# A graph network on one core: the fourth edge stage with gathered queries, two sum banks and no loop

## What is computed

```python
q = (tfn_features @ Wq).reshape(n, H, DQK)              # 8 heads of 16
x_dst = tfn_features[edge_dst]
wk = mlp2(edge_features, k_w1, k_b1, k_w2, k_b2)        # per edge, 128 wide
wv = mlp2(edge_features, v_w1, v_b1, v_w2, v_b2)
k = tensor_product(x_dst, edge_sh, wk, Cqk)             # wk * sum_s sh[s] * (x @ C[:, s])
v = tensor_product(x_dst, edge_sh, wv, Cv)              # 9 harmonics s
attn = jnp.einsum('ehd,ehd->eh', q[edge_src], k)
ex = jnp.exp(attn - segment_max(attn, edge_src)[edge_src])
alpha = ex / (segment_sum(ex, edge_src)[edge_src] + 1e-16)
upd = segment_sum(v * alpha[..., None], edge_src)
out = tfn_features @ W_self + upd.reshape(n, OV) @ W_out
return (out - mu) * jax.lax.rsqrt(var + EPS_BN) * gamma + beta
```

## Time and profile before

| | us |
|---|---|
| median of three runs | 3519.25 |
| lowest and highest | 3516.62, 3521.51 |
| the profiled execution, its own time | 3510.65 |
| its span in the profile | 3508.9 |
| mean granted TensorE clock over the span | 0.805 |

### The profile page before, as it was taken

One profiled execution on the slowest core, in us unless ns is written; L12 is line 12 of the kernel. 1 busy time (PEld: TensorE's weight loads), 2 busy tenths in 40 slices (PEclk: granted clock), 3 DMA queues, 4 the chain that ended last, 5 costly groups with the idle time before them and its releaser, 6 DMA issues. The chain is left out here.

```text
span 3508.9 us, 58176 instructions
## 1 busy us (share of the span) xinstructions
PE 2551.3 (73%) x14132; PEld 2166.8 (62%) x14132; DVE 2280.8 (65%) x5044; ACT 1062.1 (30%) x2723; POOL 1789.0 (51%) x1813
## 2 busy tenths in 40 slices
PE   3778777514554444357777765999999999999986
PEld 2778776413443333245555544888888888888872
DVE  3555555337887887855556542677777777777775
ACT  1111111134554564111111101344444344443441
POOL 2777776066666663157777723444444344443400
PEclk7776777556555666589999967999999999999985
DMA  2443443265554552035445517988888888888830
GB/s 64 93 87 84 87 87 64 46 161 131 132 123 125 132 124 72 2 110 157 153 153 161 158 63 177 203 204 197 197 201 199 200 198 190 193 200 198 195 92 9
DMA packets 433884, 475.50 MB, mean 136 GB/s; under 512 B 200837, under 2 KB 304648, under 8 KB 433712
## 3 DMA queue, kind: packets, MB, share of 16 engines
q1 hardware_dynamic: 358832, 295.60, 35.9%
q0 software_dynamic: 59904, 123.64, 15.2%
q10 hardware_dynamic: 14976, 54.53, 4.5%
HBM read 408.18 MB, written 65.34 MB: 135 GB/s over the span
## 5 line engine op out<-in xcount | busy, mean ns | idle before, releaser
L1960 PE MATMUL psum<-ckv,z 128*128 128x256 f32 x4160 | 969.7, 384 | 0.0
L1960 PEld LDWEIGHTS psum<-ckv,z 128*128 128x128 f32 x4160 | 767.9, 191 | 98.5
L1823 POOL DMA_INDIRECT ga<-XX,src_i x416 | 398.1, 957 | 449.7 <-PE psum L1941 307.0
L985 POOL DMA_INDIRECT ga<-T,src_i x416 | 431.4, 1037 | 302.3 <-issue 112.5
L275 POOL DMA_INDIRECT ga<-T,src_i x416 | 401.3, 965 | 151.7 <-issue 124.4
L275 POOL DMA_INDIRECT ga<-TA,src_i x416 | 412.4, 991 | 126.7 <-issue 126.7
L2009 DVE TENSOR_TENSOR z<-psum,shb 128x2560 f32<-128x2560 f32 x104 | 293.7, 2824 | 125.8 <-PE psum L1941 78.5
L455 PE MATMUL psum<-wre,re 128*128 128x68 f32 x832 | 213.4, 349 | 142.1 <-DVE oneT L331 82.6
L1816 POOL TENSOR_TENSOR acc<-acc,wkv 128x512 f32<-128x512 f32 x104 | 114.3, 1099 | 332.7 <-DMA wkv<-WKV 316.4
L455 PEld LDWEIGHTS psum<-wre,re 128*128 128x128 f32 x832 | 173.4, 258 | 162.9 <-issue 153.9
L2050 DVE TENSOR_TENSOR acc<-acc,psum 128x256 f32 x416 | 175.4, 422 | 120.2 <-PE psum L1932 90.9
(11 more groups left out here) (349 smaller groups left out, 4862.8 us busy)
## 6 DMA issues: line engine op xcount, KB each, us to landing
shb<-in_ea SPq DMA_DIRECT2D x104, 640.0 KB
WKV<-wkvo ACTq DMA_DIRECT2D x104, 512.0 KB
shb<-in_ea SPq DMA_DIRECT2D x104, 512.0 KB
wkv<-WKV SPq DMA_DIRECT2D x104, 512.0 KB
dl<-DL SPq DMA_DIRECT2D x312, 128.0 KB, 3.5
acc<-QW SPq DMA_DIRECT2D x416, 64.0 KB
win<-TB SPq DMA_DIRECT2D x416, 32.0 KB
ga<-T,src_i POOLq DMA_INDIRECT x832
```

What stands on the lines that cost most here:

```text
L985: pool.indirect_dma_start(ga[:, ring(g) + t, :], None, T1, bass.IndirectOffsetOnAxis(ap=src_i[:, g * GT + t:g * GT + t + 1], axis=0)).then ...
L1823: pool.indirect_dma_start(ga[:, (g % GR) * GT + t, :], None, XX, bass.IndirectOffsetOnAxis(ap=src_i[:, g * GT + t:g * GT + t + 1], axis=0) ...
L1960: last = pe.matmul(kv_of(k)[:, t, :], z[:, k % 2, j, t * 128:(t + 1) * 128], ckv[:, j, :], start=(j == 0), stop=(j == NZ - 1))
```

## The change

Queries: SyncE's `dl` and window loads go, and with them ScalarE's `places` and `queries` and TensorE's `queries`. GpSimd instead gathers each edge's row of QW by its destination, one indirect DMA a tile, into `qg`, a ring of four groups (QR), one group behind the XX gathers. GpSimd's multiply goes; VectorE makes it at the head of `keys_and_values`. The destinations of padding edges are clamped to 0 ahead of the stage. Sums: half 1 goes to bank 1, which the queries leave free, and each half waits only for the adds of the same half of the group before. Loop: `each_step` writes all 14 rounds out on every engine that used it. The diff, its removed and added lines with some of their surroundings:

```diff
@@ -1678,7 +1678,7 @@
-        QW = dram("QW", [NW, F])
+        QW = dram("QW", [N, F])
@@ -1697,13 +1697,12 @@
-                sp.dma_start(QW[N:NW, :], zero[:, 0:F]).then_inc(n3_o, 16)
-                sp.dma_start(QW[0:N, :].rearrange("(j p) f -> p j f", p=PN), tab[:]).then_inc(n3_o, 16)
-                sp.wait_ge(n3_o, 4 * 16)
+                sp.dma_start(QW.rearrange("(j p) f -> p j f", p=PN), tab[:]).then_inc(n3_o, 16)
+                sp.wait_ge(n3_o, 3 * 16)
             @block.gpsimd
@@ -1728,6 +1727,7 @@
             def _(dve):
+                c.link(dve.tensor_scalar(dst_i[:], dst_i[:], 0, None, ALU.max))
             @block.scalar
@@ -1756,14 +1756,13 @@
-        WR = 2
-        e3_w = [sem(f"e3_w{k}") for k in range(WR)]
+        QR = 4
+        e3_gq = [sem(f"e3_gq{k}") for k in range(UG)]
-        e3_dl = [sem(f"e3_dl{k}") for k in range(2)]
-        (e3_one, e3_oa, e3_oT, e3_ta, e3_X, e3_z, e3_Q, e3_q, e3_wq, e3_V, e3_ev, e3_s, e3_S, e3_acc, e3_M, e3_Mx, e3_i,
-         e3_pad, e3_sp) = [sem("e3_" + x) for x in
-            ("one", "oa", "oT", "ta", "X", "z", "Q", "q", "wq", "V", "ev", "s", "S", "acc", "M", "Mx", "i", "pad", "sp")]
+        (e3_one, e3_oa, e3_X, e3_z, e3_wq, e3_V, e3_ev, e3_s, e3_S, e3_acc, e3_M, e3_Mx, e3_i, e3_pad) = [
+            sem("e3_" + x) for x in
+            ("one", "oa", "X", "z", "wq", "V", "ev", "s", "S", "acc", "M", "Mx", "i", "pad")]
@@ -1771,7 +1770,6 @@
-        dl = tmp("dl3", [128, 2, GT * W], BF16)
@@ -1783,12 +1781,12 @@
-        oneT = acc[:, 2, 0:2 * GT * W].rearrange("p (a e) -> p a e", a=2)
-        qs = acc[:, 2, 2 * GT * W:4 * GT * W].rearrange("p (a e) -> p a e", a=2)
-        win = acc[:, 2, 4 * GT * W:4 * GT * W + WR * GT * F].rearrange("p (t f) -> p t f", f=F)
+        qg = acc[:, 2, 0:QR * GT * F].rearrange("p (t f) -> p t f", f=F)
+        sums_of = lambda half: bank[1] if half else bank[6]
+
         def soft_1(i, k):
@@ -1801,19 +1799,19 @@
         def each_step(eng, body):
-            each_group(eng, body)
-            for k in range(UG):
-                body(NI, k)
+            for i in range(NI + 1):
+                for k in range(UG):
+                    body(i, k)
             @block.gpsimd
             def _(pool):
-                def weighted_query(g):
-                    slot = g % 2
-                    pool.wait_ge(e3_q, g + 1)
-                    pool.wait_ge(e3_n[slot], (g // 2 + 1) * 16)
-                    q = qs[:, slot, :].rearrange("p (t f) -> p t f", t=GT)
-                    pool.tensor_tensor(q, q, wkv[:, slot, :, 0:F], ALU.mult).then_inc(e3_wq, 1)
+                def queries(g):
+                    if g >= QR:
+                        pool.wait_ge(e3_ev, (g - QR + 1) * 2)
+                    for t in range(GT):
+                        pool.indirect_dma_start(qg[:, (g % QR) * GT + t, :], None, QW, bass.IndirectOffsetOnAxis(
+                            ap=dst_i[:, g * GT + t:g * GT + t + 1], axis=0)).then_inc(e3_gq[g % UG], 16)
                 groups = NT // GT
                 for g in range(groups):
@@ -1822,19 +1820,15 @@
-                    if g > GR:
-                        weighted_query(g - GR - 1)
-                for g in range(groups - GR - 1, groups):
-                    weighted_query(g)
+                    if g:
+                        queries(g - 1)
+                queries(groups - 1)
             @block.sync
             def _(sp):
                 def weights_load(i, k):
-                    wait(sp, e3_wq, g - 1)
-                    sp.sem_inc(e3_sp, 1)
-                    sp.sem_inc(e3_sp, 1)
@@ -1842,14 +1836,9 @@
                     if lag(i, k, 0):
-                        wait(sp, e3_oT, g - 1)
-                        sp.sem_inc(e3_sp, 1)
-                        sp.dma_start(dl[:, k % 2, :], DL[:, cols].partition_broadcast(128)).then_inc(e3_dl[k % 2], 16)
                         wait(sp, e3_z, g - 1)
-                        sp.sem_inc(e3_sp, 1)
                         sp.dma_start(shb[D:128, k % 2, 0:NZ - 1], A["ea9"][1:NS:2, cols].partition_broadcast(D)).then_inc(e3_e[k % 2], 16)
-                        window_loads(win, sp, i, k, QW, F, e3_w, e3_Q, e3_sp, ring=WR)
@@ -1857,21 +1846,6 @@
             @block.scalar
             def _(act):
-                def queries(i, k):
-                    g = i * UG + k
-                    act.wait_ge(e3_Q, g + 1)
-                    wait(act, e3_ev, (g - 1) * 2)
-                    act.activation(qs[:, k % 2, :], bank[1][:], ACT.Copy).then_inc(e3_q, 1)
-
-                def places(i, k):
-                    g = i * UG + k
-                    act.wait_ge(e3_dl[k % 2], i * (UG // 2 * 16) + (k // 2 + 1) * 16)
-                    wait(act, e3_Q, g - 1)
-                    o = oneT[:, k % 2, :]
-                    act.activation(o, dl[:, k % 2, :], ACT.Abs, bias=iota_p[:, 0:1], scale=-1.0).then_inc(e3_ta, 1)
-                    act.wait_ge(e3_ta, g + 1)
-                    act.activation(o, o, ACT.Relu, bias=ones_c[:, 0:1], scale=-1.0).then_inc(e3_oT, 1)
-
                 def one_hots(i, k):
@@ -1898,12 +1872,8 @@
                 def body(i, k):
-                    if lag(i, k, 1):
-                        queries(*lag(i, k, 1))
-                    if lag(i, k, 0):
-                        places(i, k)
@@ -1923,13 +1893,13 @@
+                        pe.wait_ge(e3_acc, SPARE + (g * 8 - 4))
+                    else:
-                    else:
-                        pe.wait_ge(e3_acc, SPARE + (g * 8 + 4))
                     for t in range(2 * half, 2 * half + 2):
-                        pe.matmul(bank[6][:, o:o + 128], M3[:, k % 2, t, :], one[:, k % OR * GT + t, :], start=True, stop=True)
-                        last = pe.matmul(bank[6][:, o + 128:o + 256], D3[:, k % 2, t, :], ob[:, k % 2, t * W:(t + 1) * W],
+                        pe.matmul(sums_of(half)[:, o:o + 128], M3[:, k % 2, t, :], one[:, k % OR * GT + t, :], start=True, stop=True)
+                        last = pe.matmul(sums_of(half)[:, o + 128:o + 256], D3[:, k % 2, t, :], ob[:, k % 2, t * W:(t + 1) * W],
@@ -1940,16 +1910,6 @@
-
-                def queries(i, k):
-                    g = i * UG + k
-                    pe.wait_ge(e3_w[k % WR], i * (UG // WR * 64) + (k // WR + 1) * 64)
-                    pe.wait_ge(e3_oT, g + 1)
-                    wait(pe, e3_q, g)
-                    for t in range(GT):
-                        last = pe.matmul(bank[1][:, t * 128:(t + 1) * 128], oneT[:, k % 2, t * 128:(t + 1) * 128],
-                                         win[:, (k % WR) * GT + t, :], start=True, stop=True)
-                    last.then_inc(e3_Q, 1)
                 def products(i, k, t):
@@ -1970,8 +1930,6 @@
                     if lag(i, k, 0):
-                    if kv:
-                        queries(*kv)
@@ -2012,12 +1970,15 @@
                 def keys_and_values(i, k):
                     s, kk = k // KG, k % KG
+                    dve.wait_ge(e3_gq[k], i * 64 + 64)
+                    dve.wait_ge(e3_n[k % 2], i * (UG // 2 * 16) + (k // 2 + 1) * 16)
+                    q = qg[:, k % QR * GT:(k % QR + 1) * GT, :]
+                    dve.tensor_tensor(q, q, wkv[:, k % 2, :, 0:F], ALU.mult).then_inc(e3_wq, 1)
-                    dve.tensor_tensor(three(kt), kv_of(k)[:, :, 0:F], three(qs[:, k % 2, :]), ALU.mult).then_inc(e3_ev, 1)
-                    dve.wait_ge(e3_n[k % 2], i * (UG // 2 * 16) + (k // 2 + 1) * 16)
+                    dve.tensor_tensor(three(kt), kv_of(k)[:, :, 0:F], q, ALU.mult).then_inc(e3_ev, 1)
@@ -2047,7 +2008,7 @@
-                        dve.tensor_tensor(a, a, bank[6][:, (t % 2) * 256:(t % 2 + 1) * 256].rearrange("p (r n) -> p r n", r=2),
+                        dve.tensor_tensor(a, a, sums_of(half)[:, (t % 2) * 256:(t % 2 + 1) * 256].rearrange("p (r n) -> p r n", r=2),
                 def exponents(c, q, s):
```

## The result

In the measurement of the change the changed kernel takes 3381.86 us in the median (3378.82 to 3383.73), the kernel before 3517.93 (3509.2 to 3521.51): a ratio of 0.9616, with a 95% interval of 0.9597 to 0.9635. The forecast was 3407 with a range of 3380 to 3450, so the saving was 136 us where 112 had been forecast. Later comparisons ran on three chips on which the kernel before itself is slower (3841 to 3862 us), and there the same changed kernel is slower than the kernel before (ratio 1.0795).

A forecast was written before the change was run, and what follows sets the result against it. TensorE's instruction stream was taken to bound the fourth edge stage. Savings of 60.8 (cycle), 42.9 (loop), 8 (banks) and 0 (gathers, prologue) made 112 us, off the 3519.25 median: 3407, range 3380 to 3450.

The forecast's parts named there:

- B: Second plain step of the fourth edge stage's four-step cycle; forecast 10.40 us on TensorE, 8.7 on VectorE.
- C: Step of the fourth edge stage's cycle that takes softmax maxima; forecast 10.98 us on TensorE, 11.6 on VectorE.
- What VectorE gets: Fourth edge stage: VectorE gains the query multiply, regains time from shorter L617 and L598; 42.4 us a cycle, bounds 41.5 to 45.0.
- D: Step of the fourth edge stage's cycle that takes softmax exponents; forecast 10.98 us on TensorE, 13.4 on VectorE.
- A: First plain step of the fourth edge stage's four-step cycle; forecast 10.44 us on TensorE, 8.7 on VectorE.
- The cycle after: Four steps, fourth edge stage: VectorE's lag costs TensorE 1.19 us; cycle falls from 46.36 to 43.8, saving 60.8 us.
- Written out: Fourth edge stage: removing loop entry and jumps saves all 42.9 us, bounds 20 and 43, with no fetch stalls.
- Gathers on GpSimd: Fourth edge stage: eight gathers a group take 10.1 to 10.4 us, 40.5 to 41.5 a cycle, below 43.8; no bound.
- Rival 1: Fourth edge stage: TensorE stays the only bound, VectorE's lag stays inside 2.65 us; cycle 42.80, time 3382; chance 0.15.
- Rival 3: Fourth edge stage: fetch stalls replace the jumps, 20 of the 42.9 us come back, time 3427; chance 0.08.
- rivals 2 and 5: Fourth edge stage: VectorE becomes the bound, 3437 to 3482 (chance 0.20); or gather waits keep time within 7 us (0.03).
- Rival 4: Fourth edge stage: GpSimd's gathers set the pace, slower than before above 1.505 us each; about 3583 at 1.6; chance 0.06.

## Why the prediction was right, and where not

**Queries leave TensorE: right.** Steps B and C, which wait for nothing on TensorE, are 10.40 and 10.98 long in the timeline above, as forecast (10.40, 10.98). ScalarE fell from 496.93 to 336.76 us of 1185 and that bought nothing that shows.

**What VectorE gets: 42.4 forecast, 41.96 measured.** Less its waits for TensorE, the usual steps of the trace are A 8.75, B 9.12, C 11.13 and D 12.96. The multiply itself is right: 0.69 in the steps shown, forecast 0.688. Its follower starts 0.09 us behind its end, so that it takes 0.78 of a step where 0.73 was forecast. C and D were forecast at 11.6 and 13.4, 0.4 too long each. In C that is mostly L598, which took 1.11 in the step that the forecast was worked out from and takes 0.43 now, 0.68 less where 0.4 was credited. In D the working was wrong: the step it read (13.11) had L617 at 0.23 already, as it says, so that there was no 0.4 to return there, and without it D would have been 13.7. What D got back stands elsewhere, in the adds (L2045, L2050, now L2006, L2011). From L617 to the next large product it took 5.36 us and takes 4.77; one L2045 beside GpSimd's multiply fell from 0.47 to 0.19. Timeline, VectorE, before and after:

```profile
2663.76 0.23 DVE L617 TENSOR_SCALAR fdiag<-delta_t,cm 128x16 f32<-128x16 f32 x1
...
2664.77 0.47 DVE L2045 TENSOR_TENSOR acc<-acc,fac 128x2 f32 x1 [0.34 <-DVE ex L2055]
```

```profile
2656.00 0.23 DVE L617 TENSOR_SCALAR fdiag<-delta_t,cm 128x16 f32<-128x16 f32 x1
...
2656.98 0.19 DVE L2006 TENSOR_TENSOR acc<-acc,fac 128x2 f32 x1 [0.32 <-DVE ex L2016]
```

So D's 13.4 came near in part by luck: 0.5 was credited there, and 0.9 came back, from other instructions. The lower bound of 41.5 for the sum has no working behind it. Over the stage no L617 or L598 is long any more. Single lines, VectorE, to be read against the earlier trace rows:

```profile
L598 DVE TENSOR_TENSOR_SCAN lrow<-prow,crow x26: 428/429/430, 2210.3 to 3285.1; 1x136 f32<-1x136 f32 x26
...
L617 DVE TENSOR_SCALAR fdiag<-delta_t,cm x26: 222/229/323, 2220.6 to 3291.4; 128x16 f32<-128x16 f32 x26
```

The reason that I gave, GpSimd's multiply gone, holds for the long ones: before, 16 of 26 L617 and 18 of 26 L598 were long (over 0.3 and 0.5 us), each of them beside L1816. But it doesn't say how many there are. In the kernel before written out that multiply is still there, and the medians are short:

```profile
L617 DVE TENSOR_SCALAR fdiag<-delta_t,cm x26: 226/228/1142, 2546.5 to 3691.0; 128x16 f32<-128x16 f32 x26
...
L598 DVE TENSOR_TENSOR_SCAN lrow<-prow,crow x26: 428/429/1349, 2535.3 to 3684.9; 1x136 f32<-1x136 f32 x26
```

Here 6 of 26 L617 and 9 of 26 L598 are long, again all beside the multiply. Whether the two meet is a matter of how the engines stand to each other; that the loop's jumps had made them meet more often is likely but not shown, as this trace is from another chip. The rule of the Trainium skill that I cited (SBUF — State Buffer, Who interferes with whom) fits the long instances; how often it bites can't be had from it.

**The cycle after: 43.8 forecast, 43.19 measured.** The mechanism is the one told: D makes VectorE late, A and B make it up, TensorE loses in front of the sums of A. The size was off, by the D that was 0.4 too long and the C. The lag at A is 3.13 in the cycle shown and 2.83 in most, 3.84 forecast. The sums of A start 2.96 us after its transposes in most cycles and 3.27 in the one shown, where those of B, which wait for nothing, start after 2.60: TensorE loses 0.4 to 0.7 instead of 1.19. Cycle 42.80 + 0.4 = 43.2. Saved: 75.3 us for the 60.8 forecast, which is most of what the sum missed.

**Written out: 42.9 forecast, 38.2 measured.** 4.6 us remain above whole cycles, in waits of VectorE for shb (10.8 us, 6 times, of which 3.8 us lie within the 95 steps) and in cycles like the one above that take 43.49. VectorE also waited for wkv, 2.1 us in four waits up to 2239 us. The prediction had named a wait for qg or wkv as a sign of being wrong; for qg there is none. The kernel before written out gives 36.7, and 41.9 in its 95 steps. No fetch stall shows: VectorE's issue gaps in front of the large product fall from 35.3 to 0.2 us. The Trainium skill's page that I cited (Runtime: NRT & Kernel Launch, Instruction fetch mechanics) holds here, in that the straight code stalls nobody. On the other chips the loop put back costs 91 us (1.1017 against 1.0795), with its jumps inside a disturbed stage.

**Separate banks: 8 forecast, 7.1 measured** (133.3 to 126.2 from last transposes to end). The seven waits for the adds, 10.2 us in the earlier trace rows, are gone; in their place TensorE waits 12.1 us for VectorE's values in the same stretch:

```profile
PE psum L1901 <- DVE edge_a L1994: 12.1, 6, 3.1
```

VectorE, which now has the multiply, is what the drain waits for; that this kept it from giving back more is likely and wasn't tested.

**Prologue: nothing forecast, 3.0 measured**, inside the bounds of 4. The remaining 5.9 us lie ahead of the stage and are no part of the change's working.

**Gathers on GpSimd: right on the first chip.** L1813 takes 0.956 us and L1821 0.959 with 0.30 of issue, 1.26 apart, within the forecast of 1.25 to 1.30. Eight are 10.1 a group, and GpSimd waits 75.5 us for VectorE. The load of the DMA engines was forecast at 82% and is 91% in the steady part: queue 1 keeps 70.7% of their time though it moves a tenth less a microsecond (156 MB in 1000 us, 174 in the earlier trace rows), so that its time doesn't go by its bytes as the working had it. It bounded nothing beyond the waits for shb and wkv named above.

**The rivals.** Rival 1 (TensorE the only bound, 3382) gives the measured time to the microsecond, and for the wrong reason: its cycle would be 42.80, and the trace shows 43.19 with a loss in A, 9.3 us over 23.75 cycles, which other things made up. The account of the 25.4 us by which the measured time lies under the forecast (3407.25 unrounded) is: 14.5 of cycle, 3.0 of prologue and 5.9 ahead of the stage, less 4.7 of loop and 0.9 of drain, 17.8 in sum. Beyond that, the profiled execution of before lay 8.6 us under its median and that of after only 0.7 under its own, so that the medians differ by 7.9 more than the spans. The terms of the forecast add up to 111.7, and it took 112; that takes the missing 0.3 back. Rival 3 falls, and so do rivals 2 and 5 on this chip: VectorE waits for TensorE in every cycle, and the time moved.

**Rival 4 is where the working was too narrow.** It had the chance of 0.06 and the sign that the other chips show, but not the mechanism: I let GpSimd pace the stage with gathers of over 1.505 us. On the other chips a gather takes its 0.94 to 0.95 us all the same, and GpSimd waits 463.6 us for VectorE. What costs there is that others go on late, since TensorE's semaphore updates come late. Nothing in the profile of before could size it: its stage has four gathers a group, and of its updates by TensorE that ended a wait none came later than 0.015 us. The sentence on the Trainium skill (DMA: Bandwidth & Descriptors, SWDGE vs HWDGE vs iDMA), that GpSimd's path is the slower one to set up, points the right way for those chips and gives neither this mechanism nor its size.

## What to carry to other kernels

Where two engines nearly tie, price a cycle by the lag that the slow step builds up and by the cover between the products and the first use of the other's result: it explained both the loss that came and its place. A loop that is jumped eleven times cost 3.2 us a jump on VectorE, and written out the stage is 37 to 38 us shorter in two traces, from two chips. Where an engine goes on late, compare the time of the semaphore update with the recorded end of its releaser before calling the releaser slow. And a change that adds software-queue gathers should be timed on more than one chip before it is kept: here the ratio turned from 0.9616 to 1.0795, where the written-out loop alone had 0.9832.

## What the runs showed of the hardware that was not expected

- Chips seem to differ by more than the changes that one times on them: the kernel before took 3518 us in the first measurement and takes 3841 to 3862 on the three later chips, within 0.7% in each comparison.
- On those three, four more gathers a group in the software queue slow the stage by 1.7 us a group when nobody needs their data, and by 4.5 (448 us over the 100 groups more that gather) when VectorE does. Their own issue doesn't slow (0.94 to 0.95 us), and the load isn't the reason: the slower of the two has the DMA engines at 0.59, the other at 0.88.
- The slowing stands in waits whose releaser had ended 2 to 13.7 us before, by the records; on the first chip this distance is 0.11 us for the same program. It is TensorE's semaphore updates that come late, several at once, while those of the other engines stay within 0.034 us of their instructions' ends.
- Whether a VectorE instruction is lengthened by GpSimd (228 to 1142 ns, 429 to 1349 ns) hangs on whether the two meet: 16 and 18 of 26 in the kernel before, 6 and 9 of 26 in it written out on another chip, none without GpSimd's multiply.
